# Attention look-up on Trainium2: one 128-column product per tile and a predicated copy in place of two 64-column products

## The reference

```python
h_src = feat[src]
h_dst = feat[dst]
hc = jnp.concatenate([h_src, h_dst], axis=-1)
hc = jnp.tanh(hc @ W_attn.T + b_attn)
e = hc @ w_out
m = jax.ops.segment_max(e, dst, num_segments=N)
ex = jnp.exp(e - m[dst])
denom = jax.ops.segment_sum(ex, dst, num_segments=N)
alpha = ex / denom[dst]
z = jax.ops.segment_sum(alpha[:, None] * h_src, dst, num_segments=N)
```

## Time and profile before

| | us |
|---|---|
| median of 3 runs | 2012.38 |
| lowest and highest run | 2007.74, 2017.11 |
| span of the profiled execution | 2533.2 |

### The profile page before, as it was taken

How to read it: one execution, slowest core, us unless ns; L and a number is a source line. 1 busy time by engine, 2 the same in 40 slices (tenths; PEclk the granted TensorE clock), 3 DMA queues, 4 the chain that set the end, 5 groups by cost and what they waited for, 6 DMA issues and landing times.

```text
span 2533.2 us, 28723 instructions
## 1 busy us (share of the span) xinstructions
PE 1374.4 (54%) x7844; PEld 1089.7 (43%) x7845; DVE 991.2 (39%) x2889; ACT 200.8 (8%) x390; POOL 1235.7 (49%) x1381
## 2 busy tenths in 40 slices
PE   4455555565621556566555651111111898879877
PEld 2455554554511456556555640000000898434423
DVE  7555554554604333334333440000000676300488
ACT  2000000000000111111111100000000111000200
POOL 1666666666672366565666677677777000000000
PEclk8766767677755555555555555555555898899989
DMA  5444343435200222222222200000000002988878
GB/s 165 150 155 153 120 152 118 150 121 168 65 1 0 68 63 66 65 62 64 66 66 64 66 21 0 0 0 1 0 0 0 0 0 103 353 335 353 326 295 336
DMA packets 154645, 272.07 MB, mean 107 GB/s; under 512 B 44030, under 2 KB 100154, under 8 KB 151546
## 3 DMA queue, kind: packets, MB, share of 16 engines
q1 hardware_dynamic: 111322, 229.57, 24.9%
q0 software_dynamic: 40064, 41.32, 6.6%
q10 hardware_dynamic: 3232, 0.82, 0.1%
HBM read 215.32 MB, written 56.29 MB: 107 GB/s over the span
## 4 chain that ended last, share of the span: by engine, by line
another core or an unknown queue 28%; PE 26%; issue 20%; DVE 14%; POOL 5%; DMA 4%; DVEq 1%; ACT 1%; SPq 1%; POOLq 0%; ACTq 0%
PE acc L987 10%; PE acc L1035 7%; POOL rings L736 5%; PE acc L1029 4%; DVE rings L1367 2%; DVE big L1826 2%; DMA big<-pairs_by_src 2%; DVE rings L1401 2%; DVE rings L1402 1%; DVE big L1391 1%; DMA rings<-local_rows 1%; PE acc L1009 1%; DMA relation_rows<-big 1%; DMA rings<-relation_rows,idx_ring 1%
## 5 line engine op out<-in xcount | busy, mean ns | idle before, releaser
L987 PE MATMUL acc<-rings 128*65 128x128 f32 x3328 | 576.1, 326 | 634.4 <-issue 459.6
L987 PEld LDWEIGHTS acc<-rings 128*65 128x65 f32 x3328 | 456.0, 168 | 709.4 <-issue 694.3
L736 POOL DMA_INDIRECT rings<-relation_rows,idx_ring x416 | 409.5, 984 | 281.9 <-issue 184.1
L736 POOL DMA_INDIRECT rings<-attention_rows,idx_ring x416 | 394.6, 948 | 305.1 <-issue 234.3
L1029 PE MATMUL acc<-attend_mem,rings 128*128 x1664 | 373.8, 411 | 266.2 <-issue 182.3
L1029 PEld LDWEIGHTS acc<-attend_mem,rings 128*128 128x128 f32 x1664 | 367.3, 328 | 273.0 <-issue 273.0
L753 POOL DMA_INDIRECT pairs_by_src<-fed_val,fed_idx x416 | 405.6, 975 | 149.4 <-issue 120.0
L1425 DVE TENSOR_SCALAR rings<-iota_bf,col_local,score 128x256 f32<-128x256 bf16 x416 | 139.4, 408 | 480.3 <-remote 371.8
L786 POOL DMA_INDIRECT big<-support_rows,ext_node x4 | 3.9, 963 | 450.6 <-DMA support_rows<-big 449.7
L1680 DVE TENSOR_TENSOR rings<-acc,rings 128x512 f32<-128x512 f32 x52 | 35.6, 684 | 352.0 <-remote 343.9
L1035 PE MATMUL acc<-big,attend_mem 128*64 128x512 f32 x700 | 163.0, 600 | 9.1 <-DMA big<-pairs_by_src 9.1
(11 more groups left out here) (279 smaller groups left out, 895.0 us busy)
## 6 DMA issues: line engine op xcount, KB each, us to landing
big<-pairs_by_src SPq DMA_DIRECT2D x54, 2048.0 KB, 12.5
pairs_by_src<-zeros SPq DMA_DIRECT2D x24, 1792.0 KB
big<-key_rows SPq DMA_DIRECT2D x52, 512.0 KB
rings<-local_rows SPq DMA_DIRECT2D x52, 256.0 KB
big<-pairs_by_src SPq DMA_DIRECT2D x12, 1024.0 KB, 12.3
rings<-relation_rows,idx_ring POOLq DMA_INDIRECT x416
pairs_by_src<-fed_val,fed_idx POOLq DMA_INDIRECT x416
rings<-attention_rows,idx_ring POOLq DMA_INDIRECT x416
```

The costliest lines, as they stand in the source:

```text
L736: pool.indirect_dma_start(ring[h][:, u, 0:width], None, table, bass.IndirectOffsetOnAxis(ap=idx_ring[h][:, u:u + 1], axis=0),).then_inc(ga ...
L987: m = pe.matmul(node_sums[:, bass.ds(at[u] * P + w * P, P)], rows[h][:, u, :], onehot[h][:, u, w * P:(w + 1) * P], start=False, stop=False ...
```

## The change

The two blocks that a tile's destinations can lie in are neighbours in attend_dst, so 128 columns from the first block's start hold both candidates side by side. The changed kernel uses one one-hot matrix per tile, of the destination's number within its block, and one product of 128 columns per tile. Each row of the result then holds the entry from the first block and that from the second. A PSUM area of two banks per half (found) takes it. A mask per edge, one where the local number is 128 or more, tells which of the two is meant: col_upper is computed once, ScalarE converts the half's columns into int32 (upper_ring), and on VectorE a predicated copy writes the second candidate over the first where the mask is set. Then the add reads the first. The local numbers that SyncE broadcasts are reduced to 0 to 127 in the preparation, which takes two instructions in place of one.

```diff
-            view, at = carve(hot_ring[h], at, [2, H * P])
+            view, at = carve(hot_ring[h], at, [H * P])
@@ PSUM
+        found = [acc[:, (4 + 2 * h) * BANK:(6 + 2 * h) * BANK] for h in range(2)]
@@ ScalarE, before the attention loop and in it, ahead of the tanh
                 copy_indices(idx_src, 0, h, idx_copied["att"])
+                act.activation(upper_ring[h][:, :], col_upper[:, h * H:(h + 1) * H], ACT.Copy).then_inc(upper_ready, 1)
...
                     act.wait_ge(bank_read, it * 2 + h + 3)
+                    if not last:
+                        act.activation(upper_ring[h][:, :], col_upper[:, bass.ds((it + 1) * (2 * H) + h * H, H)], ACT.Copy
+                                       ).then_inc(upper_ready, 1)
@@ TensorE, look_up
-                    pe.matmul(work[2 + h][:, :], zeros[:, 0:P], zeros[:, :], start=True, stop=True
-                              ).then_inc(slot_free[key], 1)
+                    for i in range(2):
+                        m = pe.matmul(found[h][:, i * BANK:(i + 1) * BANK], zeros[:, 0:P], zeros[:, :], start=True, stop=True)
+                    m.then_inc(slot_free[key], 1)
...
-                            for w in range(2):
-                                m = pe.matmul(work[2 + h][:, u * D:(u + 1) * D], onehot_t[h][:, w, u * P:(u + 1) * P],
-                                              there[:, w * D:(w + 1) * D], start=(w == 0), stop=False, skip_group_check=True)
+                            m = pe.matmul(found[h][:, u * 2 * D:(u + 1) * 2 * D], onehot_t[h][:, u * P:(u + 1) * P], there,
+                                          start=True, stop=True, skip_group_check=True)
@@ VectorE, onehot_rows
-                for w in range(2):
-                    for e in range(0, H * P, 2 * P):
-                        o = dve.tensor_scalar(onehot_t[h][:, w, e:e + 2 * P], local_ring[h][:, e:e + 2 * P],
-                                              iota_part[:, w:w + 1], None, ALU.is_equal)
-                o.then_inc(onehot_ready[key], 1)
+                dve.tensor_scalar(onehot_t[h][:, :], local_ring[h][:, :], iota_part[:, 0:1], None, ALU.is_equal
+                                  ).then_inc(onehot_ready[key], 1)
@@ VectorE, preparation
-            dve.tensor_copy(local_bf[:, :, :], row_local[:, :, :]).then_inc(rows_derived, 1)
+            then(dve.tensor_scalar(row_src[:, :, :], row_local[:, :, :], float(P), float(-P), ALU.is_ge, ALU.mult))
+            then(dve.tensor_tensor(local_bf[:, :, :], row_src[:, :, :], row_local[:, :, :], ALU.add))
+            dve.sem_inc(rows_derived, 1)
...
             dve.wait_ge(prep_taken, 7)
+            dve.tensor_single_scalar(col_upper[:, :], col_local[:, :], float(P), ALU.is_ge).then_inc(upper_known, 1)
@@ VectorE, score_step
-                    dve.tensor_tensor(msg[h][:, :, :], work[2 + h][:, :].rearrange("p (t d) -> p t d", t=H),
-                                      rows2[h][:, :, 0:D], ALU.add).then_inc(bank_read, 1)
+                    dve.wait_ge(upper_ready, it * 2 + h + 1)
+                    both = found[h].rearrange("p (t w d) -> p t w d", t=H, w=2)
+                    dve.nop(nofuse=True)
+                    dve.copy_predicated(both[:, :, 0], upper_ring[h][:, :].unsqueeze(2).to_broadcast([P, H, D]), both[:, :, 1]
+                                        ).then_inc(picked, 1)
+                    dve.wait_ge(picked, it * 2 + h + 1)
+                    dve.tensor_tensor(msg[h][:, :, :], both[:, :, 0], rows2[h][:, :, 0:D], ALU.add).then_inc(bank_read, 1)
```

More of the change, by code:

```diff
@@ L177, in gnn_kernel @@
         col_local = sb("col_local", [P, T])
+        col_upper = sb("col_upper", [P, T], BF16)
+        upper_ring = [sb(f"upper_ring{h}", [P, H], I32) for h in range(2)]
         col_weight = sb("col_weight", [P, T])
@@ L329, in gnn_kernel @@
         w_out_bank = banks[0][:, 0:D]
+        found = [acc[:, (4 + 2 * h) * BANK:(6 + 2 * h) * BANK] for h in range(2)]
+        assert H * 2 * D == 2 * BANK
         table_banks = [*banks[0:4], *banks[6:8]]
@@ L405, in gnn_kernel @@
         tanh_ready = sem("tanh_ready")
+        upper_ready = sem("upper_ready")
+        upper_known = sem("upper_known")
+        picked = sem("picked")
         rows_kept = sem("rows_kept")
@@ L1026, in look_up @@
                         for u in range(H):
-                            there = (attend_dst[:, :, :].rearrange("p b c -> p (b c)")[:, bass.ds(at[u] * D, 2 * D)])
-                            for w in range(2):
-                                m = pe.matmul(work[2 + h][:, u * D:(u + 1) * D], onehot_t[h][:, w, u * P:(u + 1) * P],
-                                              there[:, w * D:(w + 1) * D], start=(w == 0), stop=False, skip_group_check=True)
+                            there = attend_dst[:, :, :].rearrange("p b c -> p (b c)")[:, bass.ds(at[u] * D, 2 * D)]
+                            m = pe.matmul(found[h][:, u * 2 * D:(u + 1) * 2 * D], onehot_t[h][:, u * P:(u + 1) * P], there,
+                                          start=True, stop=True, skip_group_check=True)
                         m.then_inc(slot_free[key], 1)
```

## The result

The changed kernel takes 2019.2 us (median of 14 runs, 2014.4 to 2024.0) against 2013.2 us for the kernel before (14 runs beside it, 2007.7 to 2017.6). The ratio is 1.0026, 95% interval 1.0015 to 1.0037: about 5 us slower, which lies within the 0.5% that the prediction calls no change. The forecast was 2013.0.

What follows compares the result with a forecast made beforehand. GpSimd's gathers were taken to bound the attention stage: 0.8 us of preparation plus 5 of stretched gathers made 2018, less 5 for pauses 2013; forecast case 2003 to 2022, 8 in 10 from 1955 to 2026.

Steps and rivals of the forecast that it cites:

- GpSimd bounds the attention stage: Attention stage: gathers follow each other every 1.25 us, 10.0 us per half; TensorE's and VectorE's work lies beside them.
- 110 us of pauses: Attention stage of the profile before: GpSimd's idle time beyond the 0.30 us between gathers, expected to go with half TensorE's instructions.
- The sum: Whole kernel: +0.8 us preparation, +5 us stretched gathers, nothing from TensorE, so +6 or 2018; less 5 for pauses, 2013.
- The 5 us taken off for pauses: Attention stage: 8 us of the runs' waiting left to it after the relation stage's 98; the change removes 5.
- The 415 us that were "the profile's own": Whole kernel: of 521 us between profiled span and runs' median, some 415 were held to be absent from the runs.
- The gap of 106 us: Whole kernel: median 2012.4 lies 106 us above the 1906 rebuilt from GpSimd's queue, read as waiting in relation and attention stages.
- The profiled execution: Profile after the change: attention stage 525 us, span about 2430 us, as the pauses go with half of TensorE's instructions.
- TensorE's price: Attention look-up: a 128-column record takes 0.29 us, 16 records 4.7 us per half in place of 7.0.
- VectorE's price: Attention stage: one builder 0.66 us, predicated copy 0.69 us; net -1.0 us per half, beside the gathers.
- (a): Attention stage: slow TensorE stretches partly real in the runs, so halved instructions give 1956, at most 1906; chance 0.33.
- (b): Attention stage: long builder collides with GpSimd's descriptor writing each half, deciding from 0.2 us per half, up to 2040; chance 0.14.
- (c): Attention look-up: a 128-column record takes twice the time, TensorE's 7.0 us stay, 2018; counted in the forecast case, 0.53.

Runs made afterwards that it cites:

- e1: The kernel before, unaltered, timed and profiled once more on chip A: 2012.7 us, ratio 1.0005.
- e3: The changed kernel with the one builder of 1024 elements cut into four of 256, against the kernel before on chip A: 2011.8 us, ratio 1.0001.
- e5: The changed kernel with two builders of 512 elements in place of one of 1024, on chip B: 2548.6 us in one run; kernel before there 2545.1.
- e6: The changed kernel with the long builder computed twice per half, on chip B: 2533.6 us in one run; kernel before there 2545.1.
- e8: The kernel before with every look-up product issued twice, on chip B: 2615.9 us in one run; unaltered there 2545.1.
- e12: The changed kernel with every look-up product issued three times, against the kernel before on chip D: 2585.9 us, ratio 1.016.
- e10: The kernel before with only every second attention gather issued, against it unaltered on chip C: 2231.9 us, ratio 0.884.
- e2: The changed kernel, unaltered, timed again against the kernel before on chip A: 2020.3 us, ratio 1.0037.

## Why the prediction was right, and where it was wrong

**GpSimd bounds the attention stage.** Right, for both kernels on chip A: the idle time before a gather is 0.32 us in e1 and after the change, TensorE waits 359 us for the builder and the predicated copy 314 us for landings. The earlier 110 us of pauses belong to the slow stretches.

**The sum.** 0.8 us of preparation and 5 us of stretched gathers made +6; measured are +5.2 by the ratio on the first chip and +7.4 on chip A. The keys' store starts at 37.81 us after the change and 36.91 before, 0.9 later, and the first gather at 59.75 against 58.77, 1.0 later. The gathers' stretch measures 5.0 to 6.7 us against 5. e3 shows that the builder's length makes it. That the size fits is in part luck: 0.15 us a half for the new builder and 0.06 for the old ones were chosen between wide bounds, and both were too high. Measured are 0.10 to 0.14 and, in e1, under 0.01. The upper bound came from a row read wrongly: the 1.57 us of the earlier trace rows are a scatter's, not a gather's.

**The 5 us taken off for pauses.** This is the term that failed, and it is most of the distance between 2013.0 and the 2019.2 measured. On a chip without slow stretches there are no such pauses to remove. That the measured time still lies in the range says little for the sum, since the range holds every outcome without an effect.

**The 415 us that were "the profile's own".** Wrong. The step took the difference between a profiled execution (2533) and the median (2012) for a cost of profiling. On chip A a profile of the same kernel spans 2008 us and the runs take 2011; on B, C and D the runs without a profile take 2545, 2519 and 2545. So the difference belongs to the chip, or to the hour in which it was used, for each was used once. That the first profile was taken on such a chip follows from its number and its pattern; it was not recorded. The gap of 106 us had then nothing to do with pauses either. By the windows of e1 the terms of my sum were short elsewhere: the relation stage 548 and not 535, the late scatters 485 and not 450, what follows them 298 and not 260, and the first scatters with the attention table 93 and not 82; the attention stage, 525 and not 520, is the smallest of these. Two readings made them short. A scatter was priced at 1.28 us from one row, and the group of the late ones in e1 (window 1225 to 1710) has

```profile
L753 POOL DMA_INDIRECT pairs_by_src<-fed_val,fed_idx x352 | 354.8, 1008 | 113.3 <-issue 105.0 <-POOL fed_idx L745 7.6 <-DMA pairs_by_src<-fed_val,fed_idx 0.6
```

so 1.008 us and 0.32 us before it, with other instructions of GpSimd between, 1.37 us from start to start. And the sum went from the last scatter straight to the row at 2272.98, from which it took its last 260 us. In e1 that row is

```profile
1747.88 5.77 PE L1108 MATMUL acc<-fold_ident,rings 128*128 128x64 f32 x50 [0.68 <-ACT rings L860]
```

It starts 38.9 us after the last scatter has ended (1709.0), and from it to the end there are 260.3 us: the 260 were right, and the 39 before them were left out.

**The profiled execution.** A stage of 525 us was forecast and 531 came, with a span of 2012 against the 2430 forecast. The stage came out for the wrong reason: the profile landed on a chip without slow stretches. The test that the prediction set itself, whether the stage keeps its 632 us, is answered by e5 and e6, which have half the instructions on a chip with slow stretches: 623 and 611 us. The reading that fewer TensorE instructions end the pauses is wrong.

**TensorE's price.** 16 records took 3.78 us, 0.236 each, where scaling by all columns, stationary and moving, gave 0.29; the 64-column record had 0.219. Twice the moving columns cost 8% at this clock (11% against the 0.213 of e8). A half takes 3.8 us and not 4.7. None of it mattered under 10 us of gathers.

**VectorE's price.** The predicated copy took 0.696 us (0.69 forecast, from the row of the add on the same shape): nearest row, right. The builder took 0.80 us in the mean against 0.66, and 0.74 where no gather disturbed it; the line through two float32 rows was too low for it.

**The rivals.** (a), slow stretches partly real: real they are on three of the four chips, but halving the records does not end them there (e5, e6: stages of 623 and 611 us), and where the kernel before takes 2011 to 2013 us e1 and the result's profile show none, so nothing of the 1956 came. (b), the long builder collides: the mechanism is the right one and carries the whole result. It was to decide from 0.2 us per half on; it measured 0.10 to 0.14. And the gather mean was to rise by 20 ns; it rose by 12 and by 17. (c), a record twice as expensive: fell, 0.236 against 0.219.

## What to carry to other kernels

Where GpSimd's issue of indirect transfers sets the pace, as here on chip A, less work for TensorE and VectorE brings nothing, and one long VectorE instruction in place of several short ones can cost: read the mean length of the GpSimd instruction that runs beside it, to the nanosecond, times their number. Before a difference between a profile and the median is explained, profile the same kernel again on another chip: waits "for issue" that also show in stages which no edit touches are no reason for an edit. A cut of the cover (half the gathers) tells what a hidden saving could be worth. Run it on the chip that the saving is meant for: here it ran on chip C, where TensorE's late signals took most of it. Where a wait has no releaser by the profile, look at what else waits for the same semaphore and goes on at the same instant.

## What the runs showed of the hardware

The same kernel takes 2011 us on chip A (and 2013 in the first comparison) and 2519 to 2545 us on chips B, C and D. There TensorE, while GpSimd issues transfers, has stretches in which single records stand 0.7, 1.4 or 2.1 us apart, as in e12's timeline and, ahead of the record of the earlier trace rows, in the trace of the kernel before:

```profile
1062.62 0.27 PE L1029 MATMUL acc<-attend_mem,rings 128*128 x1 [1.15 <-issue]
1064.72 0.27 PE L1029 MATMUL acc<-attend_mem,rings 128*128 x1 [1.83 <-issue]
1066.14 0.27 PE L1029 MATMUL acc<-attend_mem,rings 128*128 x1 [1.15 <-issue]
```

They were absent in the attention stage of e10 and, but for 6 us, of e8, and present in e12 in spite of triple work.

A gather that has a VectorE builder of 1024 elements alone beside it takes 1.07 us (result) to 1.09 us (e2) in the mean in place of 0.94. Beside a predicated copy of 512 elements out of PSUM it takes 0.94, and beside builders of 256 it takes 0.946 (e1, 147 gathers) and 0.949 (e3, 99 gathers), with the few of 1.05 to 1.08 among them. Two builders of 512 elements are no remedy: in e5 the 25 gathers that had nothing but them beside them took 1.10 us.
